# Attention's step list in another order on all engines: V's projection behind the sixth pair, the next image's transposes last

## The reference, cut to what matters

```python
# 16 images of 256x256; three Haar levels, gated details, inverse transform -> h (16, 256, 256)
h = _L0_tok_ref(x, ...)
# attention, 16 heads of 16, over the 256 rows of each image
Q, K, V = (proj(Wq, bq), proj(Wk, bk), proj(Wv, bv))
attn = softmax(einsum('bhqd,bhkd->bhqk', Q, K) * scale)
out = einsum('bhqk,bhkd->bhqd', attn, V) -> (B, S, D) @ Wo.T + bo
h = _layernorm(h + out)
# then: top-2 mixture of 8 experts + layernorm; a cosine/cumprod block with a small network
# + layernorms; a top-1 mixture of 8 experts with capacity + layernorm
```

## Time and profile before

| what | us |
|---|---|
| median of 3 runs | 1596.23 |
| lowest, highest run | 1588.97, 1597.39 |
| the profiled execution | 1596.87 |
| its span, first to last instruction | 1595.1 |

### The profile page before, as it was taken

The page is one execution under the profiler, slowest core; times in us unless marked ns, Lnnn a source line. Parts: engine busy times, 40 slices in busy tenths (PEclk is TensorE's granted clock), DMA queues, the critical chain, the costliest instruction groups (busy, mean ns, idle before and its releaser), DMA issues.

```text
span 1595.1 us, 23616 instructions
## 1 busy us (share of the span) xinstructions
PE 1306.6 (82%) x6856; PEld 916.3 (57%) x6856; DVE 927.7 (58%) x2735; ACT 523.6 (33%) x998; POOL 697.3 (44%) x912
## 2 busy tenths in 40 slices
PE   1368978877989875999999818888888399999997
PEld 0245555554656543666667516666666266666665
DVE  6555775676676635555555546778776344444443
ACT  1024444434555431222222135555554121111111
POOL 6551444526222124545544324554454434444443
PEclk9578789789999756999999957787777699999999
DMA  6457345544575323121211052321100361110100
GB/s 161 86 100 95 61 88 115 81 76 88 119 144 118 86 81 128 61 66 61 64 62 63 22 171 80 105 93 57 57 14 21 129 232 31 30 32 29 29 19 12
DMA packets 88747, 126.33 MB, mean 79 GB/s; under 512 B 17696, under 2 KB 71598, under 8 KB 87600
## 3 DMA queue, kind: packets, MB, share of 16 engines
q1 hardware_dynamic: 68832, 85.13, 24.0%
q0 software_dynamic: 16416, 38.46, 7.8%
q10 hardware_dynamic: 3376, 1.22, 0.4%
HBM read 71.24 MB, written 31.54 MB: 64 GB/s over the span
## 4 chain that ended last, share of the span: by engine, by line
PE 58%; DVE 16%; POOL 11%; issue 6%; DMA 4%; ACT 3%; SPq 2%; ACTq 0%; DVEq 0%; POOLq 0%
PE ebank L1931 9%; PE ebank L1942 8%; PE ebank L1158 8%; PE ebank L1170 8%; PE bank L591 3%; DVE top_a_a L961 2%; PE av_bank L647 2%; PE mbank L1492 2%; PE ebank L1952 2%; PE ebank L1180 2%; PE bank L673 2%; POOL rows_d L1431 2%; PE s_bank L614 2%; POOL rstd_m_m L1407 2%; PE s_bank L635 2%
## 5 line engine op out<-in xcount | busy, mean ns | idle before, releaser
L961 DVE TENSOR_REDUCE top_a_a<-s_bank 128x4 f32<-128x1024 f32 x128 | 156.5, 1223 | 111.5 <-PE s_bank L614 108.1
L790 ACT ACTIVATE prob_a<-s_bank 128x1024 f32<-128x1024 f32 x128 | 130.4, 1019 | 77.2 <-PE s_bank L635 75.3
L1931 PE MATMUL ebank<-w,exT 128*128 x312 | 142.2, 599 | 0.7 <-ACT exT L1977 0.7
L1492 PE MATMUL mbank<-w2T_m,fhT_m 128*128 128x256 f32 x512 | 142.7, 442 | 0.0
L1942 PE MATMUL ebank<-w,ehT 128*128 x624 | 141.2, 379 | 0.9 <-ACT ehT L1985 0.9
L1158 PE MATMUL ebank<-w,exT 128*128 x284 | 135.5, 600 | 0.6 <-ACT exT L1205 0.6
L1170 PE MATMUL ebank<-w,ehT 128*128 x568 | 134.4, 380 | 0.8 <-ACT ehT L1211 0.8
L1492 PEld LDWEIGHTS mbank<-w2T_m,fhT_m 128*128 128x128 f32 x512 | 118.7, 232 | 23.1
L1117 POOL DMA_INDIRECT ex<-rows_d,tile_row x71 | 72.4, 1020 | 127.7 <-DVE ey L1244 109.3
L1942 PEld LDWEIGHTS ebank<-w,ehT 128*128 128x128 f32 x624 | 115.6, 190 | 15.7 <-issue 1.6
L525 POOL DMA_INDIRECT rows_d<-h_a,row_i_a x64 | 63.7, 995 | 135.1 <-DVE row_i_a L1046 120.1
(11 more groups left out here) (349 smaller groups left out, 2646.3 us busy)
## 6 DMA issues: line engine op xcount, KB each, us to landing
w<-in_L_ffn_W SPq DMA_DIRECT2D x16, 1024.0 KB, 10.7
qs_a<-parts_q_a SPq DMA_DIRECT2D x96, 128.0 KB, 4.5
ks_a<-parts_k_a SPq DMA_DIRECT2D x96, 128.0 KB, 6.4
w<-in_L_ffn_w SPq DMA_DIRECT2D x16, 512.0 KB, 5.7
image_a<-in_x SPq DMA_DIRECT2D x4, 1024.0 KB, 7.4
h_d<-rec_a SPq DMA_DIRECT2D x4, 1024.0 KB, 3.8
x_a<-h_d SPq DMA_DIRECT2D x16, 256.0 KB, 5.1
ya_m<-y_d SPq DMA_DIRECT2D x16, 256.0 KB, 2.8
```

The costliest lines, as they stand in the source:

```text
L790: nc.scalar.activation(prob[:, j % 4].rearrange("p g t s -> p (g t s)"), s2_bank[:].rearrange("p g s -> p (g s)"), ACT.Exp, scale=HD ** -0 ...
L961: nc.vector.tensor_reduce(top[:, j].rearrange("p g t -> p (g t)"), s1_bank[:].rearrange("p g (t s) -> p (g t) s", t=TPI), axis=AX, op=ALU. ...
L1492: last = nc.tensor.matmul(b[:, t * D:(t + 1) * D], hT[:, f, t * P:(t + 1) * P], w2T[:, f, :], start=False, stop=f == FC - 1)
L1931: last = nc.tensor.matmul(bank[1 + n % 2][:], xT[j % 2][:, ch, :], w[:, bass.ds(e, 1), at:at + 512].rearrange("p a f -> p (a f)"), start=c ...
```

## The change

The list `STEPS` is written in another order. One entry changes its stage too: shift_1, which stood near the end of a turn ("n"), now stands near the head of the next ("t"), which makes it the same image. No function changes, no step is added or removed.

```diff
@@ -301,16 +301,18 @@
         def head(k, j):
             return 8 * (j // 2) + 2 * k + j % 2
 
-        STEPS = [("ld", "n2"), ("tokin", "n2"), ("weights", "o"),
-                 ("p2_0", "t"), ("av_3", "p"), ("p1_0", "n"), ("xb", "n2"), ("rk", "o"), ("tsum", "n2"), ("q", "f"), ("rows", "o"), ("sw_1", "t"), ("qlo", "f"),
-                 ("tsm", "n2"),
-                 ("p2_1", "t"), ("p1_1", "n"), ("ot_1", "p"), ("otv_1", "p"), ("k", "f"), ("stq", "f"),
-                 ("p2_2", "t"), ("texp", "n2"), ("klo", "f"), ("av_0", "t"), ("p1_2", "n"), ("tgate", "n2"), ("tprd_0", "n2"), ("aT", "p"), ("stk", "f"),
-                 ("p2_3", "t"), ("out", "p"), ("p1_3", "n"), ("shift_0", "n"), ("res", "p"), ("tprd_1", "n2"), ("tok", "n2"),
-                 ("p2_4", "t"), ("av_1", "t"), ("sw_0", "n"), ("v", "f"), ("p1_4", "n"), ("nrm", "p"), ("tprd_2", "n2"),
-                 ("p2_5", "t"), ("ot_0", "t"), ("p1_5", "n"), ("otv_0", "t"), ("tprd_3", "n2"), ("hT", "p"),
-                 ("p2_6", "t"), ("av_2", "t"), ("p1_6", "n"), ("tprd_4", "n2"), ("lg", "p"),
-                 ("p2_7", "t"), ("xT", "n2"), ("p1_7", "n"), ("shift_1", "n"), ("route", "p"), ("tprd_5", "n2"), ("tprd_6", "n2")]
+        STEPS = [("weights", "o"), ("shift_1", "t"), ("tsum", "n2"), ("av_3", "p"),
+                 ("p2_0", "t"), ("p1_0", "n"), ("ld", "n2"), ("rk", "o"), ("tsm", "n2"), ("rows", "o"), ("q", "f"), ("qlo", "f"), ("ot_1", "p"),
+                 ("texp", "n2"), ("sw_1", "t"), ("p1_1", "n"),
+                 ("p2_1", "t"), ("k", "f"), ("stq", "f"), ("otv_1", "p"), ("p1_2", "n"), ("klo", "f"),
+                 ("p2_2", "t"), ("aT", "p"), ("tprd_0", "n2"), ("p1_3", "n"),
+                 ("p2_3", "t"), ("shift_0", "n"), ("out", "p"), ("av_0", "t"), ("res", "p"), ("tgate", "n2"), ("stk", "f"), ("p1_4", "n"),
+                 ("tprd_1", "n2"),
+                 ("p2_4", "t"), ("sw_0", "n"), ("av_1", "t"),
+                 ("p2_5", "t"), ("tprd_2", "n2"), ("nrm", "p"), ("p1_5", "n"), ("tprd_3", "n2"), ("tok", "n2"), ("tprd_4", "n2"), ("v", "f"),
+                 ("ot_0", "t"), ("hT", "p"),
+                 ("p2_6", "t"), ("tokin", "n2"), ("p1_6", "n"), ("av_2", "t"), ("tprd_5", "n2"), ("tprd_6", "n2"), ("xb", "n2"),
+                 ("p2_7", "t"), ("otv_0", "t"), ("p1_7", "n"), ("lg", "p"), ("xT", "n2"), ("route", "p")]
 
         AHEAD = {"n2": 0, "f": -1, "n": -2, "t": -3, "p": -4, "o": -5}
```

## The result

The changed kernel takes 1516.94 us (median of 4 runs, 1513.0 to 1519.01) against 1592.6 us (4 runs, 1588.32 to 1597.39) of the kernel before on the same chip: a ratio of 0.952, 95% interval 0.948 to 0.956. That is some 76 us off; the forecast was 48 off (1548 us, range 1515 to 1582). The sign and the place were right, the size was too small by over a third.

The account below looks back on a forecast made before the run. PE was taken to set the turn, losing time to waits on other engines and the lower clock behind them. Waits 49.5 us off and 9 on gave 40, plus 8 for clock: 48 off, 1548 us, range 1515 to 1582.

Parts of the forecast that it names:

- Item 1: SyncE's queue: tokin moves behind sw_0, so sw_1's DMAs skip the wait for POOL's rebuild; 12 us off, bounds 8 and 13.3.
- Item 2: PE's wait at rk for DVE's route goes, covered by steps between p1_7 and rk; 12 us off, bounds 6 and 13.4.
- Item 3: V's projection moves ahead of ot_0 and hT; waits at hT, sw_0 and aT/out shrink 4.5, 6 and 3 us.
- Item 4: DVE's weighting pieces all go ahead of p1_7, so their sums are ready earlier; 4 us off, bounds 0 and 8.
- Item 5: POOL's first analysis goes ahead of xb(0), so the first maximum comes sooner; 5 us off, bounds 0 and 7.
- Item 6: Pair matmuls wait less for DVE's maximum as nrm and otv_0 move; 3 us off, bounds 8 off and 4 on.
- Item 7: DVE's nrm waits for POOL's root after a rebuild, 3 us on; issue gaps come forward, 6 on; bounds 3 and 20.
- Clock: PE's clock is low in turns with stalls; fewer stalls take back 8 of 32 us, bounds 0 and 25.
- first rival: PE's waits move to p1_7, nrm and issue gaps instead of going, clock stays low: 19 us off, 1578 us; chance 0.22.
- rival of no effect: The order does not reach the time; load issue spaces the pairs and removed waits return as gaps: 1594 us; chance 0.06.
- the one by SP's queue: ld of images 4, 8 and 12 waits for rec's landing, holding sw_1, stq, stk and PE: 1616 us; chance 0.05.
- The rule beside the prediction: POOL's xb and DVE's weighting pieces exclude each other in two turns, making the sum some 46 us off instead of 48.

Follow-up runs that it names:

- spread version: Changed kernel with POOL's root ahead of the row DMAs in every turn and DVE's last two weighting pieces moved into the next turn: 1546.83 us, ratio 0.968.
- last experiment: Changed kernel with POOL's root ahead of the four row DMAs for images 3 and 7 alone: 1501.41 us, ratio 0.937.
- root-first run: Changed kernel with POOL's layernorm root ahead of the row DMAs in every turn: 1545.65 us, ratio 0.965.

## Why the prediction was right, and where it fell short

**What bounds the kernel.** Right: PE's waits and the clock behind them. The outcome lies inside the range, but 2 us from its end, and there partly by luck. Two terms, V's place and the maxima, brought nothing clear of noise, SP's brought half, and the gain from joined pair groups, which had no term, made up for them and more. Everything behind the attention kept its time: from its last exponential to the end, 1015.9 us before and 1013.5 after.

**Item 1, SP** (12 off). The waits fell as foretold, from 13.3 us to 0.3, and SP's for the rebuild vanished. Alone it was worth 7, undone in the changed kernel 5 to 7. What went wrong in this term is that a wait's whole length was counted as gain when another wait (h_a) stands beneath it in the same turns.

**Item 2, routing** (12 off, at most 13.4). both_a fell by 12.2 us. But undoing it costs 37. The term was short of what follows the wait: 22 us of idle time and 15 of busy time in the fifteen turns. In the turn taken apart these are ACT's late copy of attT and the clock behind it. The upper bound, the wait's own length, was not a bound.

**Item 3, V's place** (13.5 off). Wrong: 0, or up to 4 us the other way. The waits for sw_0's shift and for attT did shrink (shift_a from 8.7 to 3.9 us), but not through V: with V in its old place shift_a waits 4.5, against 4.2 in the changed kernel beside it. And the cover for h_a is real (11.5 against 14.9) without reaching the time.

**Item 4, weighting** (4 off). The sums' wait fell by 6.3 us in the two turns named (9.9 to 3.6); the other 4.4 of the 14.3 stood in the first turn, where it now lies ahead of the first maximum. The weighting turns fell from 33.7 and 33.5 us to 31.1 and 31.3, with DVE busy 30.07 of 31.28, as said ("some 30"). No run took this item alone. The spread version shows that a weighting turn gets shorter by 3.5 us or more when two pieces leave DVE, and that the next turn takes it back.

**Item 5, start** (5 off): 3.1 in the trace, first maximum at 79.29 where "before 79" was named. The two other traces have 79.84 and 79.01, and alone the item brought 2 us. **Item 6, maxima** (3 off): 17.8 us before, and 20.8, 20.0 and 17.0 in the three traces of the changed kernel, so nothing or up to 3.0 on.

**Item 7, new waits** (3 and 6 on). The place was right, the size not. The forecast did count the row DMAs: it put the root's start 17.85 us into the turn (385.71 against 367.86), and in the changed kernel it starts 18.3 us into it. It took DVE's arrival from a short turn of the kernel before, 16.1 us in; DVE now stands ready at 14.6 (339.16 less 4.91, in the turn from 319.68). So it waits 4.9 us, not 2.7, and V and the pairs hide only 1.3 us of it, not more than half. PE loses 3.62 us in each of two turns, and its clock. In the last experiment these two turns give back 13.6 us, against 3 in the sum. The first of the three turns has no root, so it has no such wait. The 6 us of issue gaps that were to come forward are not in PE's list of the first trace; the other two traces of the changed kernel have 4.4 and 3.9 us of them.

**The term that was not there.** This is what the forecast lacked. Item 6 priced the pair matmuls by their wait for DVE's maxima alone, and the forecast took PE's busy time at full clock as fixed (nine times 22.83), whatever the order. Joining the groups alone is worth 36 us in the kernel before: PE goes on 0.1 us sooner from a group that touches another, and the waits for both_a are shorter. The short turn shows it without any clock: 1.5 of its 3.95 us are busy time. The pieces don't simply add up: joining took 10.5 us from the wait for both_a, and routing takes that same wait, so 36 and 37 us overlap.

**Clock** (8 off). Nine long turns: 41.0 us shorter, 21.8 in idle and 19.2 in busy time. If 1.5 us a turn is what the short turn gained at full clock, 13.5 of the 19.2 are that and 5.7 are clock; if only the 0.8 us of the joined kernel is, the clock has 12. The forecast's 8 for the clock lies between. Per wait removed, though, the share was too low: in the last experiment one microsecond of idle time took another of busy time with it.

**Sum.** Idle time of the fifteen turns: 33.2 off where the sum of waits had 35 (40 less item 5). That these agree is luck. The waits of item 3 (shift_a, h_a and attT) came to 1.8 off where it had 13.5, and the maxima to 3.0 on where it had 3 off; against that the wait for the sums fell by 10.7 and not by 4, and the 6 us of issue gaps did not come. Busy time: 32.5 off where it had 8. The tail behind image 15's first maximum, 10.1, was not in the sum: it runs the same list.

**The rivals.** The waits did move in part (h_a 6.3 us more, the maxima up to 3.0), but short turns fell below the 23 to 24.5 us named, which the first rival, with its clock still low, does not allow. The rival of no effect and the one by SP's queue fell: ld waits at most 10.2 us, and PE's wait for shiftT's DMAs is 0.3.

**The rule beside the prediction.** xb now directly follows the root on POOL, so it meets the normalisation in the short turns and in those where a rebuild ends: DVE's two L1008 take 1.57 to 1.59 us beside it. They take 0.74 where they don't meet, as in the two turns of the last experiment. In the weighting turn it meets a piece instead, which takes 2.17 us beside xb and 1.22 alone. The Trainium skill (SBUF — State Buffer, Who interferes with whom) says that such operations exclude each other; the trace agrees. The forecast looked for it in the two weighting turns only. In short turns it costs next to nothing, with V there as cover (21.82 us) or without (21.92).

## What to carry to other kernels

Price an order by the kernel's whole chain: a wait's length is neither the most nor the least that removing it gives, since another wait may lie beneath it (SP's place: 13 us of waits, 5 to 7 of time) and the clock and the phase of later steps hang on it (routing: 12 us of waits, 37 of time). Keep groups of short matmuls such as p1 and p2 together, and look at busy time, not only at idle time, when PE's order changes. When one engine's queue serves a rare long job, reorder around it in those turns alone: the same swap brought 20 us when made in two turns, and cost 23 when made in all.

## What the runs showed of the hardware

Four indirect DMAs issued by POOL one after the other are often followed by a stretch in which DVE, ACT or both do not take up what PE has finished. It begins near the start of the fourth and ends 1.8 to 2.5 us behind that start. It was seen in most of the kernels here, in DVE's maximum (which reads PSUM alone), in ACT's exponentials and in ACT's copies, with a releaser that the profile calls "remote" or with a wait put down to PE's matmul. It is not seen in every turn, even of the same kernel: the changed kernel's short turns take 21.82 us without it, 21.82 too where only ACT is late (by 1.4 us), and mostly 22.5 where DVE is late as well (by 1.2 to 1.3 us). The Trainium skill (SBUF — State Buffer, Who interferes with whom) says that ACT never waits on anyone for SBUF, and counts a DVE reduction among the operations that do not contend; ACT's 2.30 us at 422.50 stand beside this, so if both hold, the cause is no SBUF port. What holds the two engines was not settled: the root-first run shows that moving POOL's DMAs moves the stretch, and no run changed the number of DMAs or spaced them out. So the cost of this stretch (2.57 us of PE's waiting in the turn shown of the root-first run, and the clock behind it) is read from traces and not shown by a run that takes it away.
